# Ternary experts: five PSUM banks for the inner chunks in place of three, down products four chunks behind in place of two

## The chip, the cores and the metric

One core of a Trainium2 chip runs the whole program in one launch. The metric is device microseconds of that launch, by the median of several runs. TensorE multiplies matrices into PSUM (eight banks of 512 fp32 values per partition), ScalarE and VectorE read PSUM and work elementwise, GpSimd (POOL) works elementwise on on-chip memory, SyncE (SP) issues transfers. Engines run side by side, each its own instructions in order, and meet only through semaphores.

## What is computed

Four layers on x of 128 x 64 tokens of width 128, each a cross attention and a feed-forward block, each added to x. Only the feed-forward block of layer 0 is touched, the ternary mixture of experts: one shared expert and eight routed ones, of which each token takes one.

```python
h = (x - mu) / jnp.sqrt(var + LN_EPS) * ln_gamma + ln_beta
shared_out = jax.nn.silu(jnp.einsum('btd,fd->btf', h, sw1)) @ sw2.T
probs = jax.nn.softmax(h @ router_w.T, axis=-1)
...
h1 = jax.nn.silu(jnp.einsum('btd,efd->ebtf', h, ew1))
eo = jnp.einsum('ebtf,edf->ebtd', h1, ew2)
gate = jax.nn.one_hot(top_idx, N_EXPERTS, dtype=h.dtype) * top_prob[..., None]
routed_out = jnp.einsum('ebtd,bte->btd', eo, gate)
return shared_out + routed_out
```

The weights sw1, sw2, ew1, ew2 are rounded to -1, 0, 1 times a scale. The kernel computes all nine experts for every token and multiplies each by its gate (0 for those not chosen, 1 for the shared one).

## The kernel before

The class `Experts` builds this stage; its method `run` has one function for each engine, with the order of its instructions written out by hand. `ternary_moe` is the only caller (E = 9 experts, F = 128, not gated, not paired). The fourth layer's block, `gated_moe`, has code of its own and isn't touched.

The 64 tiles of 128 tokens are taken in 16 groups of four, so a group is 512 tokens. The inner width of 9 x 256 is cut into C = 18 chunks of 128; expert ex owns chunks 2ex and 2ex + 1. For a group, TensorE does the router's product (L1413 to L1416) and then for each chunk n:

- the up product (L1432, two matmuls of 128x512, by the helper lines L288 and L291) into a bank of PSUM. It waits until ScalarE has evacuated the chunk that held the bank before: `h_ready`, L1428, three chunks back.
- ScalarE applies silu to the bank and writes h into slot n % 6 of the tile `h` (L1460).
- two chunks after an expert's second chunk (`experts_at(n, 2)`, L1434) TensorE does that expert's down product (`output`, L1396 to L1409): 8 products, listed as 16 matmuls of 128x128, from both h slots into `y_bank[ex % 2]`. Expert ex so stands behind chunk 2ex + 3; experts 7 and 8 of a group stand behind chunks 17 and 1, the latter in the next group. It waits for h of the expert's second chunk (L1398) and until VectorE has read what the bank held (`Y_read`, L1402). Nine experts are an odd number, so expert 8 of one group and expert 0 of the next have the same bank, one behind the other (`behind = 1`).
- one step later (`experts_at(n, 3)`, L1515, step 2ex + 4) VectorE multiplies the result by the expert's gates (`add`, L1490) into `part`, and POOL adds it to `acc` (L1383). Behind expert 8 stands `finish` (L1494): VectorE waits for POOL's last sum, adds to x (L1498) and takes the statistics.

VectorE also does the routing of each group: it copies and shifts the router's logits at the group's start (L1505 to L1511), ScalarE does their exp behind its silu of chunk 2 (L1462 to L1467), and at step n = 3 VectorE waits for it (`e_ready`, L1525) and runs nine short operations, each waiting for the one before (softmax and the largest, L1527 to L1529, L1549 to L1571 and L1623). At each step the gate products come first in the code, then these. The normalisation of the next group (L1535) and the split of its transposed tile (L1537) stand at steps 8 and 14; TensorE transposes behind chunk 11 (L1437), ScalarE keeps the result behind chunk 12.

The banks: up products 0, 1, 2; down products 6 and 3; router and transposes 7; 4 and 5 are used only by the gated form of the class.

Of the kernel before, what the change touches and what calls it, by code (L numbers as in the profile page):

```python
# [284 lines left out]
def product(nc, out, w, x):  # L285

    (w_hi, w_lo), (x_hi, x_lo) = w, x
    nc.tensor.matmul(out, w_hi, x_hi, start=True, stop=False)  # L288
    if w_lo is not None:
        nc.tensor.matmul(out, w_lo, x_hi, start=False, stop=False)  # L290
    return nc.tensor.matmul(out, w_hi, x_lo, start=False, stop=True)  # L291


def sweep(group):

    for j in range(NG):
        group(j, j % 2, j == 0)
# [1013 lines left out]
class Experts:  # L1311
# [22 lines left out]
    def run(self, load_weights, prepare_dve, prepare_pe, prepare_act, route, weights, weights_at, affine, row_scale):  # L1334
        c, tag, E, F, gated, R = self.c, self.tag, self.E, self.F, self.gated, self.R
        nc = c.nc
        C = self.C = self.first_chunk(E - 1) + 2
        NB = 3

        NH = next(s for s in (4, 5, 6) if {0, 1}.isdisjoint({n % s for n in range(self.first_chunk(E - 2), C)}))  # L1340
        NY = 2
        sb, sem = self.sb, self.sem
        h = sb(f"h{tag}", [F, NH, GT])
        silu = sb(f"silu{tag}", [F, NB, GT]) if gated else None
        logits = sb(f"logits{tag}", [P, G, R])
        shifted = sb(f"shifted{tag}", [P, G, 8])
        e = sb(f"e{tag}", [P, G, R])
        up_bank, y_bank, xr_bank = c.bank[3:6], [c.bank[6], c.bank[2] if gated else c.bank[3]], c.bank[7]

        def gate_bank(n, slot):  # L1350

            return c.bank[(n + slot * C) % 2] if gated else c.bank[n % NB]

        xh_ready, xt_done, xT_ready, xT_split = sem("xh_ready"), sem("xt_done"), sem("xT_ready"), sem("xT_split")
        router_done, logits_kept, shifted_ready, e_ready = (
# [8 lines left out]
        W1_hi, W1_lo, U1_hi, U1_lo, W2, WR = weights  # L1364
# [4 lines left out]
        with nc.Block() as block:  # L1369
            @block.sync  # L1370
            def _(sp):
                load_weights(sp)
# [15 lines left out]
            @block.tensor  # L1388
            def _(pe):
                pe.sem_inc(h_ready, NB)  # L1390
                if gated:
                    pe.sem_inc(silu_done, 2)
                first_group_given(pe, xh_ready, 1, xt_done, xT_ready, xT_split)
                prepare_pe(pe)

                def output(i, ex):  # L1396
                    n = self.first_chunk(ex)
                    pe.wait_ge(h_ready, i * C + n + 2 + NB)  # L1398


                    behind = 1 if E % 2 and ex == 0 else NY
                    pe.wait_ge(Y_read, i * E + ex - behind + 1 + NY)  # L1402
                    for t in range(G):
                        for j in range(2):
                            last = nc.tensor.matmul(y_bank[ex % NY][:, t * D:(t + 1) * D],  # L1405
                                                    h[:, (n + j) % NH, t * P:(t + 1) * P],
                                                    W2[:, 2 * ex + j, :], start=(t == 0 and j == 0),
                                                    stop=(t == G - 1 and j == 1), skip_group_check=True)
                    last.then_inc(Y_done, 1)  # L1409

                def group(i, slot, first):
                    pe.wait_ge(xT_split, 2 * i + 2)
                    for t in range(G):  # L1413
                        last = nc.tensor.matmul(xr_bank[:, t * R:(t + 1) * R], c.xT[slot][:, t * P:(t + 1) * P],
                                                WR[:, :], start=True, stop=True)
                    last.then_inc(router_done, 1)  # L1416
                    x_parts = c.xT_hi[slot][:, :], c.xT_lo[slot][:, :]
                    for n in range(C):
                        w_lo = None if W1_lo is None else W1_lo[:, n, :]
                        if first and n in weights_at:  # L1420
                            pe.wait_ge(*weights_at[n])
                        if gated:
                            pe.wait_ge(silu_done, i * C + n + 1)
                            product(nc, gate_bank(n, slot)[0:F, :], (W1_hi[:, n, :], w_lo), x_parts)


                        behind = C % NB if n < C % NB else NB
                        pe.wait_ge(h_ready, i * C + n - behind + 1 + NB)  # L1428
                        if gated:
                            last = product(nc, up_bank[n % NB][0:F, :], (U1_hi[:, n, :], U1_lo[:, n, :]), x_parts)  # L1430
                        else:
                            last = product(nc, gate_bank(n, slot)[0:F, :], (W1_hi[:, n, :], w_lo), x_parts)  # L1432
                        last.then_inc(H_done, 1)
                        for back, ex in self.experts_at(n, 2):  # L1434
                            if not (back and first):
                                output(i - back, ex)
                        if n == xt_chunk:  # L1437
                            pe.wait_ge(logits_kept, i + 1)
                            transpose_group(nc, pe, c, xr_bank, i + 1, xh_ready, xt_done)

                sweep(group)
                for n in range(2):
                    for back, ex in self.experts_at(n, 2):
                        if back:
                            output(NG - 1, ex)
                keep_warm(nc, c, c.bank[0], 18)

            @block.scalar
            def _(act):
                prepare_act(act)  # L1450

                def group(i, slot, first):
                    for n in range(C):
# [5 lines left out]
                        else:  # L1459
                            nc.scalar.activation(h[:, n % NH, :], gate_bank(n, slot)[0:F, :], ACT.Silu,  # L1460
                                                 scale=row_scale[:, n:n + 1]).then_inc(h_ready, 1)
# [17 lines left out]
            def _(dve):  # L1479
# [22 lines left out]
                def group(i, slot, first):  # L1502
                    ch = Chain(dve, chain, i, self.chain_length)
                    dve.wait_ge(router_done, i + 1)
                    nc.vector.tensor_copy(logits[:, :, :], xr_bank[:, 0:G * R].rearrange("p (t r) -> p t r", t=G))\  # L1505
                        .then_inc(logits_kept, 1)
                    dve.wait_ge(logits_kept, i + 1)
                    ch.link(nc.vector.reduce_max(self.top[:, :], logits[:, :, 0:8], AX.X))
                    nc.vector.tensor_tensor(shifted[:, :, :], logits[:, :, 0:8],
                                            self.top[:, :].unsqueeze(2).to_broadcast([P, G, 8]), ALU.subtract)\  # L1510
                        .then_inc(shifted_ready, 1)  # L1511
                    routing = route(nc, ch, e, slot)
                    for n in range(C):

                        for back, ex in self.experts_at(n, 3):  # L1515
                            if not back:
                                add(i, slot, ex)
                            elif not first:
                                (finish if ex == E - 1 else add)(i - 1, 1 - slot, ex)
                        if gated:  # L1520
                            dve.wait_ge(silu_done, i * C + n + 3)
                            nc.vector.tensor_tensor(h[:, n % NH, :], up_bank[n % NB][0:F, :], silu[:, n % NB, :],
                                                    ALU.mult).then_inc(h_ready, 1)
                        if n == 3:
                            dve.wait_ge(e_ready, i + 1)  # L1525

                        for _ in range(({3: 3, 4: 7, 5: 7, 6: 7} if gated else {3: 9}).get(n, 0)):  # L1527
                            if routing:
                                routing.pop(0)()  # L1529
                        if first and n in (4, 6):  # L1530
                            scale_steps.pop(0)()
                        if i == 12 and n in (12, 16):
                            next_steps.pop(0)()
                        if n == xt_chunk - 3:
                            normalise_group(nc, dve, c, i + 1, xh_ready, xt_done)  # L1535
                        if n == xt_chunk + 3:
                            split_transposed(nc, dve, c, i + 1, 1 - slot, xT_ready, xT_split)  # L1537
                    assert not routing
                    ch.close()

                sweep(group)
                normalise_group(nc, dve, c, NG + 1, xh_ready, xt_done)
                for n in range(3):
                    for back, ex in self.experts_at(n, 3):
                        if back:
                            (finish if ex == E - 1 else add)(NG - 1, 1, ex)

# [1068 lines left out]
```

## Time and profile before

| | us |
|---|---|
| median of 3 runs | 3556.98 |
| the runs | 3566.01, 3553.40, 3556.98 |
| the profiled execution, its own time | 3553.94 |
| its span, first to last instruction | 3552.1 |
| TensorE busy in the span | 3419.6 |
| VectorE, ScalarE, POOL busy | 2472.9, 2034.0, 1245.8 |
| the ternary stage, first router matmul to last down matmul | about 403 to 846 |
| granted TensorE clock, mean | 0.99 |

In the rows, PE is TensorE's matmul part and PEld its weight loads, which overlap matmuls; ACT is ScalarE, DVE is VectorE. L and a number is a line of the kernel below. A row of the timeline gives start, length, engine, line, operation with its output and inputs, and in brackets how long the engine was idle before, and the releaser. "bank" is any bank of PSUM, "hM" the tile h of this stage. A busy TensorE is not TensorE at its peak; "issue" as a releaser means that the engine waited for nothing that the profile shows.

### The profile page before, as it was taken

To read this page: it belongs to the slowest core of one execution; us is meant where nothing else is said; L and a number is where in the kernel's file an instruction comes from. 1 tells how busy PE (TensorE), PEld (TensorE's weight loads), DVE (VectorE), ACT (ScalarE), POOL (GpSimd) and SP (SyncE) were. 2 spreads that over 40 slices of the span, in tenths; PEclk is the share of its full clock that TensorE was granted. 3 is DMA by queue.
4 is the path that set the end of the run, shared out by engine and by line. 5 is a ranking of instruction groups with operands and counts; after the bars stand their busy time and mean duration, and the time that the engine had idled before them with its cause. 6 is when DMAs were issued, how large, how long until landed. Compare 5 with 4: busy or idle time off the path is not lost. (4 is left out here: it accounts for less than half of the span.)

```text
span 3552.1 us, 99860 instructions
## 1 busy us (share of the span) xinstructions
PE 3419.6 (96%) x43551; PEld 2817.6 (79%) x43551; DVE 2472.9 (70%) x4946; ACT 2034.0 (57%) x3467; POOL 1245.8 (35%) x923
## 2 busy tenths in 40 slices
PE   7999899999999899999999999999999998999999
PEld 5888788888888555788888878878888887777777
DVE  8977555555667799666666667766666666777776
ACT  4445555554667688455555545555555555566564
POOL 1232133334554233222222223322222224555555
PEclk9999999999999999999999999999999999999999
DMA  3000000001000000000000000010000000000000
GB/s 110 11 11 11 1 1 1 1 1 38 15 15 9 1 1 1 22 7 9 7 7 9 5 22 1 1 47 9 7 7 9 7 5 1 7 7 13 7 7 13
DMA packets 15488, 41.03 MB, mean 12 GB/s; under 512 B 2959, under 2 KB 4687, under 8 KB 14158
## 3 DMA queue, kind: packets, MB, share of 16 engines
q1 hardware_dynamic: 15054, 34.64, 3.2%
q8 instruction: 345, 5.65, 0.6%
q14 instruction: 89, 0.73, 0.1%
HBM read 30.44 MB, written 4.19 MB: 10 GB/s over the span
## 5 line engine op out<-in xcount | busy, mean ns | idle before, releaser
L708 ACT ACTIVATE projL<-bank 128x512 f32<-128x512 f32 (+1 forms) x640 | 372.2, 603 | 647.5 <-PE bank L291 631.7
L511 POOL TENSOR_TENSOR probL<-probL,invL 128x1024 f32<-128x1024 f32 x160 | 304.8, 1905 | 1198.7 <-DVE invL L821 1198.7
L1706 POOL TENSOR_TENSOR h_loM<-hM,h_hiM 126x512 fp32r<-126x512 f32 x224 | 290.8, 1298 | 253.6 <-ACT h_hiM L1835 251.0
L598 PEld LDWEIGHTS bank<-valuesL,probTL 64*64 64x64 f32 x10240 | 277.7, 133 | 60.2 <-issue 54.4
L810 DVE TENSOR_REDUCE neg_maxL<-bank 128x16 f32<-128x1024 f32 x160 | 195.9, 1224 | 185.0 <-PE bank L617 153.0
L598 PE MATMUL bank<-valuesL,probTL 64*64 64x128 f32 x10240 | 316.4, 272 | 4.4 <-ACT probTL L718 4.4
L1405 PEld LDWEIGHTS bank<-w2T,hM 128*128 128x128 f32 x2304 | 277.3, 192 | 38.8 <-ACT hM L1460 23.7
L1405 PE MATMUL bank<-w2T,hM 128*128 128x128 f32 x2304 | 283.9, 277 | 15.7 <-ACT hM L1460 15.7
L1460 ACT ACTIVATE hM<-bank,ahead_scales 128x512 f32<-128x512 f32 x288 | 184.0, 685 | 189.1 <-PE bank L291 188.8
L825 DVE COPY valuesL<-bank 128x512 f32<-128x512 f32 x320 | 213.1, 679 | 106.9 <-PE bank L291 102.3
L818 DVE TENSOR_REDUCE totalL<-probL 128x16 f32<-128x1024 f32 x160 | 194.8, 1217 | 123.1 <-ACT probL L723 122.8
L1383 POOL TENSOR_TENSOR accM<-accM,partM 128x512 f32<-128x512 f32 x128 | 165.3, 1292 | 297.1 <-DVE partM L1490 297.1
L1947 DVE TENSOR_TENSOR tM<-bank,siluM 126x512 f32<-126x512 f32 x224 | 154.1, 688 | 115.1 <-PE bank L291 62.1
L713 ACT ACTIVATE valuesL<-bank 128x512 f32<-128x512 f32 x320 | 195.3, 611 | 54.8 <-PE bank L291 54.1
L1835 ACT ACTIVATE h_hiM<-hM 126x512 fp32r<-126x512 f32 x224 | 140.6, 628 | 132.7 <-DVE hM L1971 131.5
L718 ACT ACTIVATE probTL<-bank 128x512 f32<-128x512 f32 x320 | 189.0, 593 | 25.1 <-PE bank L577 25.0
L813 DVE TENSOR_TENSOR probL<-bank,neg_maxL 128x1024 f32<-128x1024 f32 x160 | 195.9, 1224 | 5.5
L1829 ACT ACTIVATE siluM<-bank 126x512 f32<-126x512 f32 x224 | 132.3, 590 | 94.8 <-PE bank L291 93.1
L1490 DVE TENSOR_TENSOR partM<-bank,gatesM 128x512 f32<-128x512 f32 x128 | 88.4, 690 | 128.4 <-PE bank L1405 127.2
L723 ACT ACTIVATE probL<-probL 128x1024 f32<-128x1024 f32 x160 | 169.4, 1059 | 2.9 <-DVE probL L813 2.8
L577 PEld LDWEIGHTS bank<-ident,probL 128*128 128x128 f32 x1280 | 150.0, 141 | 24.5 <-POOL probL L511 1.8
L577 PE MATMUL bank<-ident,probL 128*128 128x128 f32 x1280 | 167.3, 273 | 0.5 <-POOL probL L511 0.3
(309 smaller groups left out, 9063.4 us busy)
## 6 DMA issues: line engine op xcount, KB each, us to landing
ct0L<-in_ctxP SPq DMA_DIRECT2D x24, 192.0 KB, 2.5
ct1L<-in_ctxP SPq DMA_DIRECT2D x24, 192.0 KB, 2.5
x<-in_x SPq DMA_DIRECT2D x4, 1024.0 KB, 11.0
out<-x SPq DMA_DIRECT2D x8, 512.0 KB, 2.6
nct<-in_ctxP SPq DMA_DIRECT2D x16, 192.0 KB, 2.4
ahead_second<-in_L0w SPq DMA_DIRECT2D x2, 1152.0 KB, 18.2
ahead_second<-in_L3gate SPq DMA_DIRECT2D x1, 882.0 KB
ahead_second<-in_L3up SPq DMA_DIRECT2D x1, 882.0 KB
```

Of the source, the lines that this page charges most:

```text
L511: nc.gpsimd.tensor_tensor(segments(prob[:, slot, :]), segments(prob[:, slot, :]), per_segment(inv[:, slot, :]), ALU.mult).then_inc(prob_re ...
L577: last = nc.tensor.transpose(rot.bank(step, f"T{half}")[:, u * P:(u + 1) * P], prob[:, prob_slot, cols], c.ident[:, :])
L598: last = nc.tensor.matmul(o_bank[b * SEQ:(b + 1) * SEQ, t, u * D:(u + 1) * D], probT[t * SEQ:(t + 1) * SEQ, 2 * s + u, b * SEQ:(b + 1) * SEQ],
L708: nc.scalar.activation(proj[:, u, :], rot.bank(step, f"P{u}")[0:rows, :], ACT.Copy, scale=scale if paired and u % 2 == 0 else 1.0).then_in ...
L713: nc.scalar.activation(values[:, step % 4, u, :, :].rearrange("p h d -> p (h d)"), rot.bank(step, f"V{u}")[:, :], ACT.Copy).then_inc(Veven ...
L718: nc.scalar.activation(probT[:, 4 * half:4 * half + 4, :].rearrange("p s q -> p (s q)"), rot.bank(step, f"T{half}")[:, :], ACT.Copy).then_ ...
L810: nc.vector.tensor_reduce(neg_max[:, prob_slot, :], segments(s_bank.rearrange("p h c -> p (h c)")), axis=AX.X, op=ALU.max, negate=True).th ...
L813: nc.vector.tensor_tensor(segments(prob[:, prob_slot, :]), segments(s_bank.rearrange("p h c -> p (h c)")), per_segment(neg_max[:, prob_slo ...
L818: nc.vector.tensor_reduce(total[:, prob_slot, :], segments(prob[:, prob_slot, :]), axis=AX.X, op=ALU.add).then_inc(total_ready, 1)
L825: nc.vector.tensor_copy(values[:, step % 4, u, :, :].rearrange("p h d -> p (h d)"), rot.bank(step, f"V{u}")[:, :]).then_inc(Vodd_kept, 1)
L1405: last = nc.tensor.matmul(y_bank[ex % NY][:, t * D:(t + 1) * D], h[:, (n + j) % NH, t * P:(t + 1) * P], W2[:, 2 * ex + j, :], start=(t == ...
L1706: nc.gpsimd.tensor_tensor(h_lo[:, a % SLOTS, :], h[:, a % 3, :], h_hi[:, a % SLOTS, :].bitcast(F32), ALU.subtract).then_inc(lo_ready, 1)
```

## The change

The up products get five banks (0, 1, 2, 4, 5) in place of three, the number of h slots is written as 6, which it was before, the second down bank keeps its number (3), and the down products and gate products of an expert move two chunks later: `LAG` = 4 on TensorE (`experts_at(n, LAG)`: behind chunk 2ex + 5) and `LAG + 1` on VectorE (step 2ex + 6). So experts 7 and 8 of a group stand behind chunks 1 and 3 of the next group on TensorE, and experts 6, 7 and 8 at steps 0, 2 and 4 of it on VectorE. Routing stays at step 3, everything else where it was.

```diff
--- before.py
+++ after.py
@@ -1335,9 +1335,7 @@
         c, tag, E, F, gated, R = self.c, self.tag, self.E, self.F, self.gated, self.R
         nc = c.nc
         C = self.C = self.first_chunk(E - 1) + 2
-        NB = 3
-
-        NH = next(s for s in (4, 5, 6) if {0, 1}.isdisjoint({n % s for n in range(self.first_chunk(E - 2), C)}))
+        NB, NH, LAG = 5, 6, 4
         NY = 2
         sb, sem = self.sb, self.sem
         h = sb(f"h{tag}", [F, NH, GT])
@@ -1345,11 +1343,12 @@
         logits = sb(f"logits{tag}", [P, G, R])
         shifted = sb(f"shifted{tag}", [P, G, 8])
         e = sb(f"e{tag}", [P, G, R])
-        up_bank, y_bank, xr_bank = c.bank[3:6], [c.bank[6], c.bank[2] if gated else c.bank[3]], c.bank[7]
+        h_banks = c.bank[0:3] + c.bank[4:6]
+        y_bank, xr_bank = [c.bank[6], c.bank[3]], c.bank[7]
 
         def gate_bank(n, slot):
 
-            return c.bank[(n + slot * C) % 2] if gated else c.bank[n % NB]
+            return h_banks[n % NB]
 
         xh_ready, xt_done, xT_ready, xT_split = sem("xh_ready"), sem("xt_done"), sem("xT_ready"), sem("xT_split")
         router_done, logits_kept, shifted_ready, e_ready = (
@@ -1427,11 +1426,11 @@
                         behind = C % NB if n < C % NB else NB
                         pe.wait_ge(h_ready, i * C + n - behind + 1 + NB)
                         if gated:
-                            last = product(nc, up_bank[n % NB][0:F, :], (U1_hi[:, n, :], U1_lo[:, n, :]), x_parts)
+                            last = product(nc, h_banks[n % NB][0:F, :], (U1_hi[:, n, :], U1_lo[:, n, :]), x_parts)
                         else:
                             last = product(nc, gate_bank(n, slot)[0:F, :], (W1_hi[:, n, :], w_lo), x_parts)
                         last.then_inc(H_done, 1)
-                        for back, ex in self.experts_at(n, 2):
+                        for back, ex in self.experts_at(n, LAG):
                             if not (back and first):
                                 output(i - back, ex)
                         if n == xt_chunk:
@@ -1439,8 +1438,8 @@
                             transpose_group(nc, pe, c, xr_bank, i + 1, xh_ready, xt_done)
 
                 sweep(group)
-                for n in range(2):
-                    for back, ex in self.experts_at(n, 2):
+                for n in range(LAG):
+                    for back, ex in self.experts_at(n, LAG):
                         if back:
                             output(NG - 1, ex)
                 keep_warm(nc, c, c.bank[0], 18)
@@ -1512,14 +1511,14 @@
                     routing = route(nc, ch, e, slot)
                     for n in range(C):
 
-                        for back, ex in self.experts_at(n, 3):
+                        for back, ex in self.experts_at(n, LAG + 1):
                             if not back:
                                 add(i, slot, ex)
                             elif not first:
                                 (finish if ex == E - 1 else add)(i - 1, 1 - slot, ex)
                         if gated:
                             dve.wait_ge(silu_done, i * C + n + 3)
-                            nc.vector.tensor_tensor(h[:, n % NH, :], up_bank[n % NB][0:F, :], silu[:, n % NB, :],
+                            nc.vector.tensor_tensor(h[:, n % NH, :], h_banks[n % NB][0:F, :], silu[:, n % NB, :],
                                                     ALU.mult).then_inc(h_ready, 1)
                         if n == 3:
                             dve.wait_ge(e_ready, i + 1)
@@ -1540,8 +1539,8 @@
 
                 sweep(group)
                 normalise_group(nc, dve, c, NG + 1, xh_ready, xt_done)
-                for n in range(3):
-                    for back, ex in self.experts_at(n, 3):
+                for n in range(LAG + 1):
+                    for back, ex in self.experts_at(n, LAG + 1):
                         if back:
                             (finish if ex == E - 1 else add)(NG - 1, 1, ex)
```

With five banks the wait of an up product (`behind`, unchanged code) is for the h of five chunks back from chunk 3 on, and of three chunks back for chunks 0 to 2 of a group, since 18 % 5 = 3.

## Rows read from the trace of the kernel before

**Rows 1.** The page, part 1: busy time, share of the span, instructions, by engine.
```profile
PE 3419.6 (96%) x43551; PEld 2817.6 (79%) x43551; DVE 2472.9 (70%) x4946; ACT 2034.0 (57%) x3467; POOL 1245.8 (35%) x923
```

**Rows 2.** Groups by line, 400 to 850 us; busy us, mean ns, idle before.
```profile
L1405 PE MATMUL bank<-w2T,hM 128*128 128x128 f32 x2304 | 283.9, 277 | 15.7 <-ACT hM L1460 15.7
...
L1460 ACT ACTIVATE hM<-bank,ahead_scales 128x512 f32<-128x512 f32 x288 | 184.0, 685 | 189.1 <-PE bank L291 188.8
```

**Rows 3.** Waits, 400 to 850 us: engine, line, awaited; total us, times, longest.
```profile
PEld bank L1405 <- ACT hM L1460: 23.7, 19, 1.5
...
PEld bank L1405 <- issue: 5.2, 15, 0.3
...
PE bank L288 <- ACT hM L1460: 2.5, 3, 1.0
```

**Rows 4.** Timeline, an ordinary pair of chunks: start us, us, engine, line, operation.
```profile
610.70 0.48 PE L288 MATMUL bank<-xT_hi,w1T 128*128 128x512 f32 x1
...
611.72 1.95 PE L1405 MATMUL bank<-w2T,hM 128*128 128x128 f32 x16
...
613.42 0.48 PE L288 MATMUL bank<-xT_hi,w1T 128*128 128x512 f32 x1
```

**Rows 5.** Timeline, front of group 8, 628.3 to 636 us.
```profile
628.37 0.48 PE L288 MATMUL bank<-xT_hi,w1T 128*128 128x512 f32 x1
...
628.65 0.69 DVE L1490 TENSOR_TENSOR partM<-bank,gatesM 128x512 f32<-128x512 f32 x1 [1.58 <-PE bank L1405]
...
629.48 2.02 PE L1405 MATMUL bank<-w2T,hM 128*128 128x128 f32 x16
...
630.72 0.69 DVE L1498 TENSOR_TENSOR x<-accM,x 128x512 f32<-128x512 f32 x1 [1.39 <-POOL accM L1383]
631.11 0.23 ACT L1464 ACTIVATE eM<-shiftedM 128x32 f32<-128x32 f32 x1
...
631.26 0.48 PE L288 MATMUL bank<-xT_hi,w1T 128*128 128x512 f32 x1
...
631.36 1.28 ACT L1460 ACT_TABLE_LOAD   x1
...
632.65 1.84 ACT L1460 ACTIVATE hM<-bank,ahead_scales 128x512 f32<-128x512 f32 x3
...
632.86 0.18 DVE L1567 TENSOR_REDUCE totalM<-eM 128x4 f32<-128x32 f32 x1
...
633.40 2.05 PE L1405 MATMUL bank<-w2T,hM 128*128 128x128 f32 x16 [0.96 <-ACT hM L1460]
...
634.85 0.69 DVE L1490 TENSOR_TENSOR accM<-bank,gatesM 128x512 f32<-128x512 f32 x1
...
635.20 0.48 PE L288 MATMUL bank<-xT_hi,w1T 128*128 128x512 f32 x1
```

**Rows 6.** Timeline, group 0, 401 to 437 us.
```profile
410.46 0.23 ACT L1464 ACTIVATE eM<-shiftedM 128x32 f32<-128x32 f32 x1
...
410.73 0.19 DVE L1567 TENSOR_REDUCE totalM<-eM 128x4 f32<-128x32 f32 x1 [5.10 <-ACT eM L1464]
...
420.46 0.50 PE L288 MATMUL bank<-xT_hi,w1T 128*128 128x512 f32 x1 [1.04 <-ACT hM L1460]
```

**Rows 7.** TensorE gaps and windows (busy us by engine, then clock PEclk, DMA, GB/s).
```profile
463.00:490.00 27.00, 26.05 (x193) 23.85 (x192) 14.12 (x39) 14.86 (x22) 10.31 (x8) 1.00 0.00 1
...
1192.00:1194.00 2.00, 2.00 (x4) 0.87 (x3) 2.00 (x3) 2.00 (x6) 1.09 (x2) 0.50 0.00 0
1194.00:1196.00 2.00, 2.00 (x11) 1.48 (x10) 2.00 (x3) 2.00 (x6) 0.65 (x1) 0.68 0.00 0
...
2965.00:2968.00 3.00, 3.00 (x18) 2.41 (x17) 1.77 (x3) 0.77 (x2) 2.54 (x2) 1.00 0.00 0
...
1191.48 1.68 PE L2049 MATMUL bank<-pG,ident 128*128 128x512 f32 x2 [2.59 <-DVE ppart L2170]
...
2964.81 0.64 PE L1733 MATMUL bank<-ident,gatesM 128*96 128x128 f32 x4 [1.73 <-DVE gatesM L1916]
```

## The prediction

> **What bounds the kernel now.** I read the page's first part first: TensorE has work in 96% of the span, VectorE in 70%, ScalarE in 57% [rows 1]. So TensorE sets the pace, and what the change can bring or cost is time in which TensorE stands still inside the ternary stage, or that it newly stands still. The groups by line, cut to that stage, show the parts: 2304 down matmuls, 288 evacuations on ScalarE of 0.685 us (184 us in a stage of some 440) [rows 2]. ScalarE is free more than half of the stage, so it can't bound it on average; only a delay at one place can. The waits say which: the down products wait for h from ScalarE (23.7 us by their weight loads, 19 times) and for 15 times 0.35 us, 5.2 us in all, on something that the profile does not name [rows 3].
>
> The timeline of group 8 gives both places. I call the chunks of a group c0 to c17. An ordinary pair of chunks takes 2.72 us: the products start at 610.70, the next pair's at 613.42 [rows 4]. In group 8, c2 starts at 628.37, c4 at 631.26 (2.89, so 0.17 over) and c6 at 635.20 (3.94, so 1.22 over) [rows 5]. The first excess is the unnamed wait: the down product of expert 0, behind c3, goes into the bank of expert 8, since nine experts on two banks put two neighbours on one; VectorE reads expert 8 from 628.65 to 629.34 and the matmul starts at 629.48. The second is the silu/exp change of tables: after c2's silu, ScalarE loads a table, does the exp (0.23) and loads the silu table again (1.28 each), and h of c3, the first of three silus from 632.65, is there only at about 633.34; the down product of expert 1, which stands behind c5, starts at 633.40 instead of about 632.3. Together 1.39 to 1.40 us per group; other groups show the same steps.
>
> **The change part by part.**
>
> Nothing is added or removed: the same matmuls, evacuations, gate products, exp and table loads. The down product of expert ex moves from behind chunk 2ex+3 to behind 2ex+5, the gate product on VectorE from step 2ex+4 to 2ex+6. No DMA and no SP or POOL instruction moves; POOL's sums follow VectorE's.
>
> *Later down products.* Expert 1 now follows c7 and finds h of c3 long done. The 1.22 us goes, in every group that has it.
>
> *Five banks.* The product of c5 waits for h of c0 in place of c2. In steady groups that wait is not late now (the products wait for h 3 times in the whole stage, all in group 0 [rows 3]), so I cost it at nothing; what covers it is ScalarE's spare time between the evacuations, and no step takes that away. It pays in group 0 alone, below.
>
> *What is late next.* At the front of a group VectorE's order is fixed: step 3 waits for e and does nine chained routing operations, and the gate products stand at even steps. Before, expert 8 of the old group was read at step 2, ahead of routing. Now it is read at step 4, behind it. And TensorE's down product of expert 0, now behind c5, still wants that read, as it goes into the same bank. So TensorE waits for ScalarE's exp and VectorE's routing, which nobody on TensorE waited for before. The step in group 8's times [rows 5], with c2 at 628.37 as before since nothing ahead of it changes (down of expert 7 replaces that of 8 behind c1):
> - exp ends at 631.11 + 0.23 = 631.34. ScalarE's order up to it is unchanged.
> - VectorE starts routing 0.04 us later, as it did in group 0, where it was waiting for it (exp ends 410.69, routing starts 410.73) [rows 6]. In group 8 it is now held by exp alone: the finish of the old group, which held routing to 632.86, comes behind it.
> - routing to gate product: 634.85 - 632.86 = 1.99. So the read of expert 8 runs from 633.37 for 0.69 to 634.06.
> - 0.14 to the matmul (629.34 to 629.48): down of expert 0 starts at 634.20. With no wait it would start at about 632.1.
> - down to next product after a stall: 635.20 - 633.40 = 1.80. So c6 starts at 636.00.
>
> c2 to c6 is then 7.63 us against 6.83 before and 5.44 without any stall. Each of the 15 groups after the first loses 0.80 us: two stalls of 1.39 go and one of 2.19 comes. That is +12.0 us.
>
> Bounds on that term: if routing were as before except that the DVE-to-TensorE release took 0.05 us, as from ScalarE (633.34 to 633.40), and the run of down matmuls lost nothing (1.70, 611.72 to 613.42 [rows 4]), it is 0.80 - 0.09 - 0.10 = 0.61 per group, +9.2 us. If the chain slips by one more 0.22 us routing pitch, it is 1.02, +15.3 us. I take 0.80, since every link has its own row.
>
> *Behind the read.* The finish of the old group (POOL's sum, x, statistics) now stands behind it: from 634.06, some 1.39 for POOL + 0.69 + 1.45 for the statistics (631.41 to 632.86), to 637.6, and delays VectorE's product of expert 0, whose down product ends about 636.3. Expert 2 needs that bank only behind c9, at about 639.7. Its read ends at 638.3, so nothing is late; if the cover went, the cost would be tenths. From c8 on I see the old order.
>
> *Group 0.* It has no old expert to read, so neither new wait. ScalarE's chain of table loads, the same in both, governs until its silu of c6; TensorE then starts c9 at 420.46 [rows 6]. With five banks and the later down products it is at c11 instead, two chunks (about 1.02 us) ahead: the one gain of the banks. It gives back some 0.2 us to the read of expert 1 and 0.3 to the normalised x for the transposes, which VectorE does behind the token scales; both are estimates from its order. I take -0.5 us, between 0 and -1.0. The down product that group 0 no longer holds is done at the stage's end, which thus costs nothing net.
>
> **Sum.** 12.0 - 0.5 = +11.5 us. The profiled execution took 3553.94 us (span 3552.1 and 1.8 around it), and becomes 3565.4. The median of the three runs shown is 3556.98, 3.0 above the profiled one, so I give 3568.5. About 0.3% (10.7 us) is what a measurement of this kernel can tell from no change; my sum lies just above it.
>
> **A rule against the row.** Both bubbles repeat in every group, and the row says one is a table load and the other a read of expert 8 [rows 5]. The Trainium skill, Perfetto Trace Analysis, section Optimization Strategy, says of consistent bubbles on the engine that should be saturated that they can mean too few SBUF or PSUM buffers. By that rule more inner banks would close them and the kernel would be faster by 1.39 x 15; this is the rival B below. The row on expert 8 names another bank than those that are added.
>
> **Rivals.**
>
> A, the forecast, +11.5 us.
>
> B, faster: routing does not stand in front of the read in time. If exp and routing were done 2.1 us earlier, or the read of expert 8 were not awaited by expert 0, both bubbles go: 15 x 1.39 + 0.5 = 21.4 us, 3535.6. For it: the 1.22 us surely goes. Against: ScalarE can't do silu of c2 before c2, and the order of VectorE is written out. It decides at the read's end: before about 631.9, B; at 634.06, A.
>
> C, no measurable difference: the new stall is nearer 1.4 than 2.2 us, because a link (release, routing, restart) is shorter than its row, or because group 0 brings its full 1.0. The sum's low end is 9.2 - 1.0 = +8.2 us, 3565. For it: the sum is only 0.8 us above the 0.3%.
>
> D, the clock: TensorE now idles from about 632.3 to 634.2, 1.9 us a group. The granted clock was 1.00 through groups with 0.96 us idle [rows 5, 7]. A gap of 1.73 before 2964.81 was survived too, the clock in 2965 to 2968 being 1.00; behind a gap of 2.59, before 1191.48, it was 0.50 from 1192 to 1194 and 0.68 in 1194 to 1196, about 3.4 us at 1.2 GHz in place of 2.4 [rows 7]. A fall costs at most half of that, 1.7 us; in all 15 groups +25.5, 3594; in some, in between. For it: 1.9 lies between 1.73 and 2.59. Against: in my gap the work on both sides is dense.
>
> E, the change does nothing as written (banks and lag both covered): 3557. The 1.22 us shows a wait that the lag must move, so I give this next to nothing.
>
> **How the numbers follow.** A 0.70, B 0.07, C (with E) 0.15, D 0.08. A holds mostly above the 0.3% line, but 0.17 of its chance lies under it once the bounds and the medians' spread are in: slower 0.53 + 0.08 = 0.61, same 0.17 + 0.15 = 0.32, faster 0.07. The range leaves out B and most of D: from C's 3565 less 5 for a median that falls nearer to the fastest run shown, 3560, to A's upper bound (3557 + 15.3 = 3572) plus 5 for the same reason, 3577.
>
> **What would show it.** In the profile after: weight loads and matmuls of the down products wait for ScalarE only in group 0; in 15 groups TensorE stands 1.9 to 2.2 us ahead of expert 0's down product, released by VectorE's gate product of expert 8, which directly follows routing; c2 to c6 is 7.6 us; routing starts 0.04 us after exp; the clock stays at 1.00. I am wrong if c2 to c6 is under 6.8 us, if the read comes ahead of routing, or if the pairs from c8 on take more than 2.72 us.

## The result, and the profile after

| | before | after |
|---|---|---|
| median, 16 runs each | 3558.27 us | 3579.40 us |
| ratio to before, 95% interval | | 1.0061 (1.0048 to 1.0074) |
| span of the profiled execution | 3552.1 us | 3575.4 us |
| ternary stage in it, router of group 0 to last down matmul | 442.7 us | 463.6 us |

The change makes the kernel 0.61% slower: 21.7 us by the ratio, 21.1 between the two medians. 11.5 us were forecast, and the forecast's range ended at 3577. The stage alone accounts for 20.9 us in the profile.

The page after the change, against [rows 1]: the same instructions, TensorE busy 10 us more.

```profile
PE 3429.8 (96%) x43551; PEld 2832.1 (79%) x43551; DVE 2474.2 (69%) x4946; ACT 2033.2 (57%) x3467; POOL 1244.2 (35%) x923
```

The waits of 400 to 868 us (engine, line, awaited; total us, times, longest), against [rows 3]; the numbers of lines are one less than before. Read the last row first: 15 times TensorE's down matmuls wait for VectorE's gate product, 1.96 us each, a wait that was not there. Routing (L1566) now waits for exp in all 16 groups, which shows that nothing else holds it. The weight loads' waits "for ScalarE" are mostly the same 15 places; ScalarE had long been done there, and the read of expert 8 came last.

```profile
PEld bank L1404 <- ACT hM L1459: 36.9, 17, 2.4
DVE totalM L1566 <- ACT eM L1463: 35.6, 16, 5.1
PE bank L1404 <- DVE partM L1489: 29.4, 15, 2.0
```

The front of group 8 (c0 to c17 are again the chunks), against [rows 5]:

```profile
635.59 0.48 PE L288 MATMUL bank<-xT_hi,w1T 128*128 128x512 f32 x1
...
636.61 1.95 PE L1404 MATMUL bank<-w2T,hM 128*128 128x128 f32 x16
...
638.34 0.23 ACT L1463 ACTIVATE eM<-shiftedM 128x32 f32<-128x32 f32 x1
...
638.60 0.18 DVE L1566 TENSOR_REDUCE totalM<-eM 128x4 f32<-128x32 f32 x1 [2.04 <-ACT eM L1463]
...
639.88 1.84 ACT L1459 ACTIVATE hM<-bank,ahead_scales 128x512 f32<-128x512 f32 x3
...
640.61 0.69 DVE L1489 TENSOR_TENSOR partM<-bank,gatesM 128x512 f32<-128x512 f32 x1
...
641.44 2.02 PE L1404 MATMUL bank<-w2T,hM 128*128 128x128 f32 x16 [1.96 <-DVE partM L1489]
642.67 0.69 DVE L1497 TENSOR_TENSOR x<-accM,x 128x512 f32<-128x512 f32 x1 [1.38 <-POOL accM L1382]
...
643.22 0.48 PE L288 MATMUL bank<-xT_hi,w1T 128*128 128x512 f32 x1
...
644.81 0.68 DVE L1489 TENSOR_TENSOR accM<-bank,gatesM 128x512 f32<-128x512 f32 x1
...
645.94 0.48 PE L288 MATMUL bank<-xT_hi,w1T 128*128 128x512 f32 x1
```

The down product of expert 8 starts behind c3 with no wait (636.61), and h of c3, ready at 640.57, delays nobody any more. Exp ends at 638.57, routing starts at 638.60, the read of expert 8 comes behind it at 640.61 and lasts to 641.30, and the down product of expert 0 starts 0.14 later, at 641.44. c2 to c6 is 643.22 - 635.59 = 7.63 us, the forecast's number to the hundredth. The finish ends at 644.8, the product of expert 0 follows, and c8 starts at 645.94, 2.72 behind c6: nothing is late behind it, as forecast.

But the groups don't all look so. From one group's first router matmul to the next, in us:

```
group      0      1      2      3      4      5      6      7      8      9     10     11     12     13     14  | tail
before  31.06  27.23  27.22  27.23  27.22  27.22  27.23  27.22  27.22  27.22  27.23  27.21  28.60  27.23  27.23 | 29.17
after   28.51  29.64  29.60  28.01  28.02  29.60  28.02  29.60  28.01  28.02  29.60  28.02  29.60  28.01  28.02 | 33.33
```

Six groups take 1.58 us more than the others, and so does group 15 (tail: its router to the last down matmul). Here is the front of group 7, first TensorE's timeline, then windows over it and over group 3 (busy us by engine, then the granted clock):

```profile
608.71 0.48 PE L288 MATMUL bank<-xT_hi,w1T 128*128 128x512 f32 x1
...
611.85 2.66 PE L1404 MATMUL bank<-w2T,hM 128*128 128x128 f32 x16 [1.96 <-DVE partM L1489]
614.16 0.77 PE L288 MATMUL bank<-xT_hi,w1T 128*128 128x512 f32 x1
...
616.01 2.17 PE L1404 MATMUL bank<-w2T,hM 128*128 128x128 f32 x16
617.93 0.48 PE L288 MATMUL bank<-xT_hi,w1T 128*128 128x512 f32 x1
```

```profile
488.00:516.00 28.00, 26.05 (x194) 24.09 (x193) 14.36 (x39) 14.83 (x23) 10.29 (x9) 1.00 0.00 1
612.00:614.00 2.00, 2.00 (x15) 2.00 (x16) 0.87 (x3) 0.13 (x1) 1.05 (x1) 0.76 0.01 4
614.00:616.00 2.00, 2.00 (x7) 1.63 (x6) 1.82 (x11) 0.60 (x1) 0.00 (x0) 0.50 0.00 0
616.00:618.00 2.00, 2.00 (x18) 1.99 (x16) 0.00 (x0) 0.77 (x2) 0.00 (x0) 0.88 0.00 0
```

Up to c5 the group is as the others. Then comes the gap of 1.96 us, and the down product behind it lasts 2.66 us in place of 2.02, the matmuls of c6 0.77 in place of 0.48: the granted clock is 0.50 in 614 to 616, 1.2 GHz in place of 2.4, and back at 2.4 GHz before 618. In group 3 (488 to 516) it is 1.00 throughout. Each of the seven falls comes behind such a gap; the other eight groups have the same gap and no fall.

### The profile page after: what moved, and what is told of

Read it like the earlier page. It is cut to its first block and busy times, and to the rows that moved or that the text cites. A ratio compares the mean times of both kernels' runs of the same rounds, so it can differ in the third digit from the quotient of the medians.

```text
span 3575.4 us, 99845 instructions
## 1 busy us (share of the span) xinstructions
PE 3429.8 (96%) x43551; PEld 2832.1 (79%) x43551; DVE 2474.2 (69%) x4946; ACT 2033.2 (57%) x3467; POOL 1244.2 (35%) x923
## 5 line engine op out<-in xcount | busy, mean ns | idle before, releaser
L1404 PEld LDWEIGHTS bank<-w2T,hM 128*128 128x128 f32 x2304 | 285.4, 196 | 48.8 <-ACT hM L1459 36.9
## 6 DMA issues: line engine op xcount, KB each, us to landing
x<-in_x SPq DMA_DIRECT2D x4, 1024.0 KB, 10.8
```

## The experiments

The theory so far: the lag puts routing ahead of the read of expert 8 (0.80 us in each of 15 groups), and the idle gap this makes lets the clock fall in seven groups (1.58 us each). The rivals: the falls, or part of the cost, come from the banks or from something else. Group lengths below are read off the first router matmul of each group, as above.

In the excerpts below "..." stands for lines left out, and the clock in a row of windows is the third number from the end.

**e1, fill the gap.** Eight matmuls into a free bank where TensorE would idle.

```diff
                         for back, ex in self.experts_at(n, LAG):
+                            if ex == 0 and not first:
+                                pe.wait_ge(logits_kept, i + 1)
+                                for _ in range(8):
+                                    nc.tensor.matmul(xr_bank, c.xT_hi[slot][:, 0:P], c.xT_hi[slot][:, :], start=True, stop=True)
                             if not (back and first):
                                 output(i - back, ex)
```

> The changed kernel with eight filler matmuls (128x512 into bank 7, which is free there) ahead of the down product of expert 0 in groups 1 to 15, 8 x 0.216 = 1.7 us put into the 1.96 us in which TensorE idles for the read of expert 8. Theory (the idle gap makes the clock fall in some groups, 1.58 us each): the groups that took 29.60 us take 28.02 like the others, the granted clock stays at 1.00 from group 1 on, and the stage is 7 x 1.58 = 11 us shorter than in the changed kernel though TensorE does more; against the kernel before +10 us, ratio 1.003. Rival (the falls come from something else in the changed kernel, its banks or its start): falls as often as before, ratio 1.006; and if the fillers only cost time, 1.007 or more.

Measured: ratio 1.0033 (1.0020 to 1.0045), stage 452.8 us, 10.8 less than after the change; groups 1 to 14 all take 28.01 or 28.02. The timeline of group 8, and the clock over all of the stage behind group 0's start:

```profile
635.74 1.53 PE L1437 MATMUL bank<-xT_hi 128*128 128x512 f32 x6
...
636.56 0.69 DVE L1493 TENSOR_TENSOR partM<-bank,gatesM 128x512 f32<-128x512 f32 x1
...
637.40 2.02 PE L1404 MATMUL bank<-w2T,hM 128*128 128x128 f32 x16
```

```profile
412.00:850.00 438.00, 434.03 (x3107) 397.12 (x3106) 229.81 (x624) 239.72 (x354) 159.91 (x124) 1.00 0.00 1
```

The fillers (the row at 635.74 is the six of them still in that window) run up to 637.3, the down product starts at 637.40, right behind the read, and the stall is as long as ever. Only the clock is different. So the falls come from the idle gap, and they are worth 11 us of the change's 21.

**e2, read expert 8 ahead of routing.** One gate product is moved from step 4 to step 3 (and to the stage's end for the last group).

```diff
                 def finish(i, slot, ex):
-                    add(i, slot, ex)
...
                         if n == 3:
+                            if not first:
+                                add(i - 1, 1 - slot, E - 1)
                             dve.wait_ge(e_ready, i + 1)
```

> The changed kernel with one gate product moved: VectorE reads expert 8 of the old group at step 3 ahead of the wait for exp and the nine routing operations, the rest of its finish stays at step 4. Theory (the 2.19 us stall is routing standing before that read, and the clock falls follow from it): c2 to c6 is 5.6 us in place of 7.63, the groups take 26.0 us in place of 28.02, no group takes 29.60, and against the kernel before it is 15 x 1.22 + 0.85 in group 0 + 1.38 in group 12 = 20.5 us faster, ratio 0.994. Rival (the order of the read doesn't matter, TensorE waits for something that comes with the lag or the banks): ratio 1.003 to 1.006.

Measured: ratio 0.9958 (0.9945 to 0.9970), stage 423.5 us, 19.2 less than before the change, groups 26.13 to 26.17 us, clock 1.00. The timeline of group 8:

```profile
614.85 0.48 PE L288 MATMUL bank<-xT_hi,w1T 128*128 128x512 f32 x1
...
617.85 0.69 DVE L1489 TENSOR_TENSOR partM<-bank,gatesM 128x512 f32<-128x512 f32 x1 [2.03 <-PE bank L1404]
...
618.46 0.18 DVE L1567 TENSOR_REDUCE totalM<-eM 128x4 f32<-128x32 f32 x1
618.62 1.27 POOL L1382 TENSOR_TENSOR accM<-accM,partM 128x512 f32<-128x512 f32 x1 [1.45 <-DVE partM L1489]
...
618.69 2.02 PE L1404 MATMUL bank<-w2T,hM 128*128 128x128 f32 x16
618.88 1.06 DVE L1569 TENSOR_TENSOR probsM<-eM,totalM 128x32 f32<-128x32 f32 x1
...
620.47 0.48 PE L288 MATMUL bank<-xT_hi,w1T 128*128 128x512 f32 x1
...
623.46 0.68 DVE L1489 TENSOR_TENSOR accM<-bank,gatesM 128x512 f32<-128x512 f32 x1
...
624.29 2.02 PE L1404 MATMUL bank<-w2T,hM 128*128 128x128 f32 x16
```

c2 (614.85) to c6 (620.47) is 5.62 us: the read at 617.85 stands ahead of routing, and only the 0.17 us of the old kernel is left. Routing ends later, but its result is needed only for the product of expert 0 at 623.46. That read is now just too late for expert 2 in the same bank (624.29, some 0.12 us), which is why the groups are 26.15 and not 26.0. The stage confirms the forecast of 20.5 less within 1.3 us. About 1.1 us of the 19.2 is not the code's doing: at the stage's start the clock was at 1.2 GHz for some 7 us in the profile of before (0.50 in 404 to 406) and never in this one (1.00 in 400 to 410). Group 0 takes 28.5 to 28.8 us in the change, e1, e5, e8 and e10, which have that stretch, and 27.54 in e2 and e7, which don't. The whole kernel gained less, 0.42%; the profiled span is 12.9 us shorter, 6 less than the stage. Segments outside the stage, whose code is the same, differ between profiles by such amounts, and for the first of them (from the narrow attention's start to the next block's) the clock goes with it: it took 317.3 us before, 321.3 in e2 and 324.4 in e5, at a granted clock of 0.98, 0.97 and 0.96. That is 4.0 of the 6 us; for the rest I have no cause.

**e3, the lag alone,** and **e4, the banks alone.**

```diff
-        NB, NH, LAG = 5, 6, 4
+        NB, NH, LAG = 3, 6, 4   # e3
+        NB, NH, LAG = 5, 6, 2   # e4
```

> The changed kernel with three inner banks (0, 1, 2) as before, down products four chunks behind. Theory (the lag alone makes the new wait, the banks pay only in group 0): groups 1 to 15 take 28.02 us or 29.60 where the clock falls, c2 to c6 7.63; group 0 loses up to 0.9 us; ratio to the kernel before 1.006, the same as the change within 0.001. Rival (the five banks 0, 1, 2, 4, 5 carry part of the cost or of the falls): ratio under 1.004.

> The changed kernel with the down products two chunks behind as before, five inner banks. Theory (the banks do nothing in steady groups): c2 to c6 6.83 us, groups 27.2 us, two stalls at the old places, no fall of the clock, ratio 1.000 (at most 1 us gained in group 0). Rival (the banks cost or pay by themselves): another ratio, over 1.002 or under 0.998.

Measured: e3 ratio 1.0068 (1.0056 to 1.0080), groups 28.01 or 29.61 (falls in groups 1, 3, 5, 8, 11, 13, and one inside group 0); e4 ratio 1.0012 (0.9998 to 1.0026), groups 27.22 and 28.60 as before the change, no fall. So the lag is the whole cost, and five banks are worth nothing in a steady group. With the lag they pay in group 0, which takes 31.13 us in e3 and 28.51 in the change: with three banks TensorE idles 2.84 us there, ahead of the fall inside the group. In e3 the gap ahead of expert 0 is 1.96 us as in the change, but other groups are hit, and six of 15 in place of seven.

**e5 and e6, a shorter gap.** The read of expert 8 stands behind seven, and behind five, of the nine routing operations.

```diff
                         if n == 3:
                             dve.wait_ge(e_ready, i + 1)
+                            for _ in range(7):
+                                routing.pop(0)()
+                            if not first:
+                                add(i - 1, 1 - slot, E - 1)
+                            while routing:
+                                routing.pop(0)()
```

> The changed kernel with the read of expert 8 behind seven of the nine routing operations in place of all nine. Both theories give the stall: c2 to c6 7.63 - 2 x 0.22 = 7.19 us, groups 27.58 us, TensorE idle 1.52 us at the place. Theory (it is the length of the idle gap that lets the clock fall, and 1.96 is just enough for some groups; elsewhere in this kernel a gap of 1.73 passed): no group with a fall, or one or two at most. Rival (any stall at this place does it, with the groups' phase): again 5 to 7 groups 1.58 us longer.

> The same with the read behind five of the nine: c2 to c6 6.75 us, groups 27.14 us, idle 1.08 us. Theory: no fall of the clock behind group 0. Rival (any stall at this place): 5 to 7 falls.

Measured, in one execution of each (3564.74 and 3549.58 us, too few to compare whole times; both on another chip than e1 to e4): e5 groups 27.56 or 27.57 (one 27.81), e6 27.11 or 27.12, and no fall in either behind group 0. The gap in e5 and the clock over its stage:

```profile
631.52 0.68 PE L1404 MATMUL bank<-w2T,hM 128*128 128x128 f32 x4 [1.50 <-DVE partM L1489]
```

```profile
412.00:846.00 434.00, 409.10 (x3013) 377.47 (x3013) 247.30 (x626) 238.51 (x352) 162.67 (x127) 1.00 0.00 1
```

The filled and the shorter gap point the same way at this place. But 1.50 us isn't a safe length in general. Ahead of the last block's first router matmul, in code that no run changed, TensorE idles 1.55 to 1.58 us, and the clock fell behind that gap in nine of the twelve profiles: in before and, on the same chip and in the same execution as the 15 gaps of 1.50, in e5. Here they are, before first:

```profile
2954.82 1.03 PE L1726 MATMUL bank<-ahead_small,xT 128*128 128x9 f32 x8 [1.58 <-PEq L264]
2956.00:2958.00 2.00, 2.00 (x7) 1.61 (x6) 1.93 (x5) 0.27 (x3) 1.65 (x1) 0.64 0.00 0
```

```profile
2965.50 1.03 PE L1728 MATMUL bank<-ahead_small,xT 128*128 128x9 f32 x8 [1.55 <-PEq L264]
2967.00:2969.00 2.00, 2.00 (x8) 1.58 (x7) 1.99 (x3) 0.56 (x3) 1.36 (x1) 0.69 0.00 0
```

**e9, a longer gap.** Two short chained copies on VectorE ahead of routing.

```diff
                             dve.wait_ge(e_ready, i + 1)
+                            for k in range(2):
+                                nc.vector.tensor_copy(pause[:, :], e[:, 0, :]).then_inc(paused, 1)
+                                dve.wait_ge(paused, 2 * i + k + 1)
```

> The changed kernel with two short chained copies on VectorE (one pitch of 0.22 us each) between the wait for exp and routing, so that the read of expert 8 comes later by about 0.4 us: TensorE idle 2.4 us, c2 to c6 about 8.05, groups without a fall about 28.45 us. Theory (the length of the gap decides how many groups see a fall: none of 15 at 1.52, 7 at 1.96): more falls than 7, say 9 or more, each about 1.6 us. Rival (the share is set by something else than the gap's length): 6 or 7 again.

Measured, in one execution (3594.24 us): groups of 28.42 and of 30.0 us; the long ones are 3, 4, 6, 8, 9, 11, 13 and 14, eight falls. I had expected nine or more. Two gaps of the same length, in group 1 without a fall and in group 3 with one:

```profile
441.56 2.02 PE L1405 MATMUL bank<-w2T,hM 128*128 128x128 f32 x16 [2.36 <-ACT hM L1460]
```

```profile
498.41 3.08 PE L1405 MATMUL bank<-w2T,hM 128*128 128x128 f32 x16 [2.37 <-ACT hM L1460]
501.14 0.77 PE L288 MATMUL bank<-xT_hi,w1T 128*128 128x512 f32 x1
```

The rows name ScalarE's h as what ended the gap, but here too it was the read of expert 8, which ends at 441.42 in group 1, 0.14 ahead of the matmul. The down product lasts 2.02 us behind the first gap and 3.08 behind the second. At this place a longer gap brought more falls (none of 15 at 1.50 us, six or seven at 1.96, eight at 2.37). But the last step adds only one, gaps of 1.55 to 1.58 us elsewhere brought a fall in nine profiles of twelve, and one of 1.64 us (from 1427.5 us on in before) in none of the twelve. So length alone doesn't decide, neither whether a fall comes nor which groups are hit.

**e10, the change once more.**

> The changed kernel itself once more, for the profile of a second execution. Theory (the falls follow from each group's idle gap and where it happens to lie in time): again 5 to 8 groups with 29.6 us among groups of 28.02, though not the same ones; outside the stage the segments differ by a few us, as they do between other executions. Rival (the falls of the first profile were chance): no or one group at 29.6.

Measured (one execution, 3581.19 us): the same seven places, groups 1, 2, 5, 7, 10, 12 and the tail, with 29.59 to 29.63 us, and a stage of 463.6 us. That the falls recur was expected, that they fall on the very same groups was not; the stage had started 2.4 us later than in the first profile. So they are no chance of one execution, though two profiles don't show that every execution has them there.

**e7, down banks in turn.** Expert ex of group i goes into bank (ex + i) % 2, so that expert 0 has not the bank of expert 8.

```diff
                 def output(i, ex):
+                    bank = y_bank[(ex + i) % NY]
...
-                    behind = 1 if E % 2 and ex == 0 else NY
+                    behind = NY
...
-                    nc.vector.tensor_tensor(out, y_bank[ex % NY][:, :].rearrange("p (t d) -> p t d", t=G),
+                    nc.vector.tensor_tensor(out, y_bank[(ex + i) % NY][:, :].rearrange("p (t d) -> p t d", t=G),
```

> The changed kernel with the two down banks taken in turn over the groups, expert ex of group i in bank (ex + i) % 2, so that expert 0 no longer shares its bank with expert 8 of the group before; order of all engines as in the change. Theory: the stall before expert 0 goes wholly (c2 to c6 5.44), no fall of the clock; VectorE is still late, as the finish of the old group stands ahead of the product of expert 0, so expert 2 (behind c9) waits about 1.0 us for that read: groups 26.9 us, and against the kernel before 15 x 0.33 + 0.85 + 1.38 = 7 us faster, ratio 0.998. Rival (TensorE is held by VectorE's order whatever the banks): c2 to c6 stays near 7.6.

Measured: groups 26.77 to 26.79 us, no fall, stage 433.0 us, 9.8 less than before (about 1.1 of it again the clock at the stage's start); ratio 1.0000 (0.9979 to 1.0021), which does not tell 0.998 from no change. TensorE in group 8:

```profile
625.83 1.95 PE L1405 MATMUL bank<-w2T,hM 128*128 128x128 f32 x16
627.53 0.48 PE L288 MATMUL bank<-xT_hi,w1T 128*128 128x512 f32 x1
...
628.55 1.95 PE L1405 MATMUL bank<-w2T,hM 128*128 128x128 f32 x16
...
632.16 2.02 PE L1405 MATMUL bank<-w2T,hM 128*128 128x128 f32 x16 [0.74 <-DVE accM L1490]
```

The down product of expert 0 starts at 625.83 + 2.72 = 628.55, unstalled, although VectorE's order is that of the change: routing ends at 627.07 and the read of expert 8 at 627.80. So the shared bank is the other half of the cause. What is late next is as expected the read of expert 0, held by the old group's finish, 0.74 us of idle before 632.16. The Trainium skill, Perfetto Trace Analysis, section Matmuls, says that independent groups of matmuls should rotate through PSUM banks so that reading one overlaps the next; with nine experts on two banks one pair doesn't rotate, and this run's 2.19 us agree.

**e8, all of it.** The change, with banks in turn (e7), the read first (e2), and the old group's statistics at step 7 in place of step 4.

```diff
                     nc.vector.tensor_tensor(xg, acc[:, :, :], xg, ALU.add).then_inc(x_done, 1)
                     dve.wait_ge(x_done, i + 1)
-                    take_stats(nc, dve, c, i, bn_done, stats_done)
+                    if last:
+                        late_stats(i)
...
+                        if n == 7 and not first:
+                            late_stats(i - 1)
```

> The changed kernel with banks in turn, the read of expert 8 ahead of routing, and the statistics of the old group at step 7 in place of step 4. Theory (all waits at a group's front are then gone): groups 25.85 us against 26.14 with the read alone, no fall of the clock, stage 419 us, against the kernel before 20.5 + 4 = 24 us faster in the stage, ratio 0.993 to 0.995. Rival (another wait is behind these): groups stay at 26.1.

Measured: groups 25.81 or 25.82 us, no fall, stage 419.6 us, 23.1 less than before; ratio 0.9955 (0.9938 to 0.9972), span 3530.2. The stage is as expected. The ratio lies just above the expected 0.993 to 0.995, which its interval overlaps. It equals e2's 0.9958 within their intervals: in whole times the last 4 us can't be told. Both beat the kernel before and the change.

## Why the prediction was wrong

- *The steady step* was right, link for link: exp, 0.04, routing 2.0, read 0.69, release 0.14, restart 1.78, c2 to c6 7.63; groups 28.02 against 27.22, 0.80 each. 15 x 0.80 = 12.0 us.
- *That nothing is late behind the read*, and *that the banks pay only in group 0*, were right (c8 at 645.94; e3, e4). Group 0 and the tail together changed by 28.51 + 33.33 - 31.06 - 29.17 = 1.61 us; without the tail's fall (1.58) and its stall (0.80), which are counted elsewhere, that is -0.8 us, against -0.5 forecast.
- *A term was missing.* In group 12 the old kernel took 28.60 us. ScalarE does a square root there for the next block's scales, between two more loads of a table, and the down product behind c17 waits 1.11 us for h, as this timeline of before shows:

```profile
756.87 1.28 ACT L330 ACT_TABLE_LOAD   x1
...
758.16 0.21 ACT L330 ACTIVATE root<-var_eps 128x8 f32<-128x8 f32 x1
...
758.39 1.28 ACT L1460 ACT_TABLE_LOAD   x1
...
760.43 1.83 PE L1405 MATMUL bank<-w2T,hM 128*128 128x128 f32 x14 [1.11 <-ACT hM L1460]
```

  The lag hides it: the group takes 28.02 + 1.58 after the change. That is -1.38 us, a gain that I overlooked, since I took the steady group for all.
- *The step that failed is rival D, the clock.* Price and place were right: 1.9 us of idle in each group, "a fall costs at most 1.7 us", measured 1.58. The sum has no term for it ("the clock stays at 1.00"), and the range left most of it out. The argument against it, that the work on both sides of the gap is dense, does not hold: seven gaps of 1.96 us between dense work let the clock fall. Of the two gaps that I compared with, 1.73 and 2.59 us [rows 7], mine lay between them, so these rows decided nothing, and a chance of 0.08 was no reading of them. And the trace of before held two shorter gaps with a fall behind them that I did not weigh: the 1.58 us ahead of 2954.82, shown at e5, and 1.80 us ahead of 394.90, just before the stage (clock 0.64 in 396 to 398, 0.51 in 398 to 400). About a half would have been a fair reading. What the runs showed: seven falls, 7 x 1.58 = 11.1 us, and with the gap filled (e1) none.

Together 12.0 - 0.8 - 1.4 + 11.1 = 20.9 us, the stage's difference. The likely case of the forecast, with the clock at 2.4 GHz, was run by e1: ratio 1.0033, 11.7 us.

- *The rule on consistent bubbles* (the Trainium skill, Perfetto Trace Analysis, section Optimization Strategy) pointed at more buffers, and rival B was built on it. e4 gave the inner chunks five banks alone and left both bubbles (groups 27.22 us, as before): the trace disagrees. The wait for the shared down bank did go in e7, but by the order of the same two banks, not by their number.
- Direction (slower, 0.61) was right, rivals B and C did not come.

What stays open: what beside its length decides whether a gap lets the clock fall, and why the same groups were hit in two executions.

## What to carry to other kernels

When work is moved later to get it out of one wait, write out the order of every engine that reads its result: here a gate product that moved by two steps fell behind a chain that waits for a third engine, and a shared bank handed that wait to TensorE. Moving that one read ahead of the chain turned +0.61% into -0.42%. And price an idle gap on TensorE by the clock as well as by its length; look up every gap of about its length in the trace before, and what the clock did behind each (here 1.58 and 1.80 us with a fall, 1.64 and 1.73 without), and give the fall a chance to match; a few filler matmuls in a gap that can't be avoided keep the clock up (e1, 11 us).

## What the hardware showed that was not expected

- A gap of 1.96 us, between stretches in which TensorE was dense, let the granted clock fall to 1.2 GHz in 7 of 15 groups (6 of 15 in e3), 2.37 us in 8 of 15, 1.50 us in none; with the gap filled (e1) in none. The same groups were hit in both profiles of the changed kernel. Elsewhere in the kernel a gap of 1.55 to 1.58 us did it in nine profiles of twelve, and one of 1.64 us in none.
- A small operation of VectorE on two on-chip tiles lasted as long as the sum of POOL that ran beside it: in e2's rows above, L1569 takes 1.06 us, to 619.94, beside POOL's sum that ends at 619.89, and so in all 15 groups that have that sum there; in the change, with POOL idle, the same operation takes 0.19. It cost nothing here, since e2 has time at that place.
